# One transformer layer with a mixture of experts on one core: three float32r passes on split operands in place of two float32 passes in the shared gate and up products

## The reference

```python
x = _layernorm(x + attention(x))
normed = _layernorm(x, ln_w, ln_b); xf = normed.reshape(-1, 256)
logits = xf @ router_w
top_idx = argmax(logits); top_score = sigmoid(max(logits))
# routed: each token goes, scaled by top_score, through the expert top_idx
shared = silu(xf @ sh_gate) * (xf @ sh_up) @ sh_down     # 256 -> 512 -> 256
x = _layernorm(x + (x + routed + shared))
```

## Time and profile before

| | us |
|---|---|
| runs before (3): lowest, median, highest | 968.13, 968.39, 968.78 |
| span of the profiled execution, first to last instruction | 966.2 |
| median minus span | 2.2 |
| TensorE busy in the span | 942.9 (98%) |
| VectorE busy | 738.7 (76%) |
| ScalarE busy | 463.9 (48%) |
| GpSimd busy | 357.6 (37%) |
| blocks of the shared expert, first gate to first expert gate | 557.2 to 762.1 |

### The profile page before, as it was taken

The page is one execution under the profiler, slowest core; times in us unless marked ns, Lnnn a source line. Parts: engine busy times, 40 slices in busy tenths (PEclk is TensorE's granted clock), DMA queues, the critical chain, the costliest instruction groups (busy, mean ns, idle before and its releaser), DMA issues. The chain is left out here.

```text
span 966.2 us, 19079 instructions
## 1 busy us (share of the span) xinstructions
PE 942.9 (98%) x6068; PEld 526.2 (54%) x6068; DVE 738.7 (76%) x1835; ACT 463.9 (48%) x648; POOL 357.6 (37%) x475
## 2 busy tenths in 40 slices
PE   9999899999999999999999899999999999999996
PEld 5555433334344333433433256666665799947996
DVE  5889899999999899999996566666666467576564
ACT  2553466666766676677666722211212232364321
POOL 8995242222222222212222324333444233333334
PEclk9999999999999999999999999999999999999999
DMA  8797444446665464855621187333316232222321
GB/s 305 191 256 206 67 67 57 57 62 89 94 100 73 58 102 54 121 74 77 141 35 13 13 266 222 112 83 88 88 50 221 74 85 80 70 57 76 99 68 45
DMA packets 174815, 98.97 MB, mean 102 GB/s; under 512 B 132480, under 2 KB 161408, under 8 KB 171520
## 3 DMA queue, kind: packets, MB, share of 16 engines
q1 hardware_dynamic: 161344, 71.85, 39.0%
q10 hardware_dynamic: 8576, 12.58, 3.9%
q0 software_dynamic: 4800, 13.38, 3.7%
HBM read 65.05 MB, written 32.31 MB: 101 GB/s over the span
## 5 line engine op out<-in xcount | busy, mean ns | idle before, releaser
L1092 ACT ACTIVATE probs<-scores_ps 128x1024 f32<-128x1024 f32 (+3 forms) x384 | 289.7, 807 | 111.3 <-PE scores_ps L1033 108.5
L302 DVE TENSOR_REDUCE maxima<-max_ps 128x1 f32<-128x512 f32 (+2 forms) x352 | 227.1, 681 | 24.7 <-PE max_ps L260 18.6
L260 PE MATMUL max_ps<-k_stack,q_stack 96*128 96x512 bf16 (+3 forms) x768 | 221.7, 329 | 3.9 <-DVE maxima L297 1.1
L1171 POOL TENSOR_SCALAR_AFFINE_SELECT probs<-probs 128x512 f32<-128x512 f32 x128 | 81.3, 636 | 303.2 <-ACT probs L1092 302.4
L1033 PE MATMUL scores_ps<-q_stack,k_stack 99*128 99x512 bf16 (+3 forms) x768 | 182.6, 326 | 2.9 <-ACT probs L1092 1.3
L1053 PE MATMUL out_ps<-probs,v_ones 128*32 128x512 f32 (+3 forms) x1536 | 163.6, 498 | 3.5 <-POOL probs L1171 3.0
L260 PEld LDWEIGHTS max_ps<-k_stack,q_stack 96*128 96x128 bf16 x768 | 74.0, 96 | 156.7 <-DVE maxima L302 60.6
L297 DVE CUSTOM_DVE_ANT_0 masked_out<-max_ps,mask_wide 128x384 bf16<-128x384 f32 (+1 forms) x256 | 149.7, 620 | 11.6 <-PE max_ps L260 7.1
L1559 ACT ACTIVATE silu<-gate_ps 128x512 f32<-128x512 f32 x68 | 40.6, 597 | 211.8 <-PE gate_ps L1460 111.3
L1033 PEld LDWEIGHTS scores_ps<-q_stack,k_stack 99*128 99x128 bf16 x768 | 66.9, 98 | 65.2 <-ACT probs L1092 15.6
L1921 POOL DMA_INDIRECT out<-out_t,target_i x36 | 45.5, 1263 | 88.7 <-DVE out_t L1851 88.7
(11 more groups left out here) (210 smaller groups left out, 1244.0 us busy)
## 6 DMA issues: line engine op xcount, KB each, us to landing
k_stack<-k_parts SPq DMA_DIRECT2D x96, 128.0 KB, 4.3
q_stack<-q_parts SPq DMA_DIRECT2D x96, 128.0 KB, 7.2
q_parts<-parts SPq DMA_DIRECT2D x32, 192.0 KB, 3.2
k_parts<-parts SPq DMA_DIRECT2D x32, 192.0 KB, 3.2
sums_in<-expert_sums SPq DMA_DIRECT2D x31, 136.0 KB, 2.1
heads_rows<-heads_out SPq DMA_DIRECT2D x128, 32.0 KB, 1.9
res<-in_x SPq DMA_DIRECT2D x8, 512.0 KB, 4.6
heads_in<-heads_rows SPq DMA_DIRECT2D x64, 64.0 KB, 3.2
```

The source lines that it names most:

```text
L260: last = nc.tensor.matmul(part, self.q_stack[:ROWS, u.slot, h0 + k, t * P:(t + 1) * P], self.k_stack[:ROWS, u.slot, h0 + k, chunk * BLOCK: ...
L302: nc.vector.tensor_reduce(self.maxima[:, u.slot, chunk, h0:h0 + heads, t], self.bank("piece", u.i, n)[:, :heads * keys].rearrange("p (h k) ...
L1092: nc.scalar.activation(probs[:, s % RING, 2 * pair:2 * pair + 2, n0:], scores_ps[:, pair, :, n0:], ACT.Exp).then_inc(exp_done, 1)
L1171: nc.gpsimd.affine_select(out=tile, in_=tile, compare_op=ALU.is_ge, fill=0.0, base=0, pattern=[[0, GROUP], [1, P]], channel_multiplier=-1) ...
```

## The change

The shared weights are loaded into two spare tiles as before. GpSimd splits them during attention units 7 to 14, a quarter of one matrix per unit, at steps 10 and 11: a rounded copy (high) and the remainder (low), both as float32r. Each block's tokens are split too: `keep_xf` writes `xf_t` as before, then `take_xf_high` on ScalarE makes a rounded copy in `xf_split`, then `leave_xf_low` on GpSimd subtracts it from `xf_t`. For block 0 VectorE does all three in the last attention unit. Gate and up then run three matmuls per half of the channels: high x high, high x low and low x high (weight x token). Four tiles share memory in new ways (`xf_t` has one copy instead of two and serves as `rows_in` later, `hidden_t` and `sums_in` lie on the gate's and up's high parts, `row` moves into `feed`), and a `memset` of `row` goes.

```diff
+HIGH, LOW = 0, 1
+THREE = [(HIGH, HIGH), (HIGH, LOW), (LOW, HIGH)]
...
     def keep_xf(self, act, copy, i, batch, odd):
         act.wait_ge(self.xf_turned, i + 1)
-        wait(act, self.up_done, BT * (i - 1))
-        copy(self.xf_t[:, odd], self.front_ps[:]).then_inc(self.xf_t_kept, 1)
+        wait(act, self.routed, i)
+        copy(self.xf_t[:], self.front_ps[:]).then_inc(self.xf_t_kept, 1)
+
+    def take_xf_high(self, act, copy, i, batch, odd):
+        act.wait_ge(self.xf_t_kept, i + 1)
+        wait(act, self.up_done, BT * i)
+        copy(self.xf_split[:, HIGH].bitcast(F32R), self.xf_t[:]).then_inc(self.high_made, 1)
+
+    def leave_xf_low(self, eng, marker, subtract, i, batch, odd):
+        eng.wait_ge(self.high_made, i + 1)
+        wait(eng, self.up_done, BT * i)
+        stand(eng, marker)
+        subtract(self.xf_split[:, LOW].bitcast(F32R), self.xf_t[:], self.xf_split[:, HIGH],
+                 ALU.subtract).then_inc(self.low_made, 1)
...
-        nc.gpsimd.memset(self.row[:], 0.0).then_inc(self.const_step, 1)
...
+    def split_shared(self, pool, n, part):
...
+        if part == HIGH:
...
+            self.nc.gpsimd.tensor_copy(high.bitcast(F32R), loaded).then_inc(self.split_step, 1)
+        else:
...
+            self.nc.gpsimd.tensor_tensor(low.bitcast(F32R), loaded, high, ALU.subtract).then_inc(self.split_step, 1)
...
                     if (u.i, s) == OPEN["turn_xf"]:
                         f.keep_xf(dve, nc.vector.tensor_copy, 0, 0, 0)
+                        f.take_xf_high(dve, nc.vector.tensor_copy, 0, 0, 0)
+                        f.leave_xf_low(dve, f.dve_stood, nc.vector.tensor_tensor, 0, 0, 0)
...
+                    if s >= STEPS - 2 and 0 <= u.i - GROUPS - 3 < 2 * f.PIECES:
+                        f.split_shared(pool, u.i - GROUPS - 3, s - STEPS + 2)
...
+            def times_xf(to_ps, weights, n):
+                for c in range(DC):
+                    for weight, token in THREE:
+                        last = nc.tensor.matmul(to_ps, weights[weight][:, c, n * P:(n + 1) * P].bitcast(F32R),
+                                                f.xf_split[:, token, c].bitcast(F32R),
+                                                start=(c == 0 and (weight, token) == THREE[0]),
+                                                stop=(c == DC - 1 and (weight, token) == THREE[-1]))
+                return last
+
             def gate(i, n, odd):
-                pe.wait_ge(xf_t_kept, i + 1)
+                pe.wait_ge(f.high_made, i + 1)
+                pe.wait_ge(f.low_made, i + 1)
                 wait(pe, silu_made, IC * i + n - 1)
...
+                times_xf(gate_ps[:, n % 2], sh_gate, n).then_inc(gate_done, 1)
...
                 if nxt is not None:
                     f.keep_xf(act, nc.scalar.copy, i + 1, nxt, 1 - odd)
+                    f.take_xf_high(act, nc.scalar.copy, i + 1, nxt, 1 - odd)
...
                     scatter_sums(i - 1, 1 - odd, range(BT - 1))
+                f.leave_xf_low(pool, pool_stood, nc.gpsimd.tensor_tensor, i, None, odd)
                 scatter_rows(i, odd)
```

More of the change, by code:

```diff
@@ L22 @@
 F32 = mybir.dt.float32
+F32R = mybir.dt.float32r
 BF16 = mybir.dt.bfloat16
@@ L621 @@
     VEC_STEPS = 17
-    CONSTS = 15
+    CONSTS = 14
+    PIECES = 4
+    SUM_RING = 3
+    SPLITS_MADE = 2 * 2 * PIECES
     def __init__(self, nc, io, keep, scratch, b):
@@ L627, in __init__ @@
         self.n = 0
-        self.sh_gate = b.sb("sh_gate_sb", [P, DC, INNER])
-        self.sh_up = b.sb("sh_up_sb", [P, DC, INNER])
+        with ExitStack() as split_ctx:
+            split = Bufs(nc, split_ctx)
+            high = [split.sb(f"sh_{name}_high", [P, DC, INNER]) for name in ("gate", "up")]
+            low = [split.sb(f"sh_{name}_low", [P, DC, INNER]) for name in ("gate", "up")]
+        self.sh_gate, self.sh_up = zip(high, low)
+        self.hidden_t = b.sb("hidden_t", [P, 2, INNER])
+        self.sums = b.sb("sums_in", [P, self.SUM_RING, RECORD])
+        b.sb("up_high_end", [P, DC * INNER - self.SUM_RING * RECORD])
+        self.sh_loaded = [b.sb("sh_gate_sb", [P, DC, INNER]), b.sb("sh_up_sb", [P, DC, INNER])]
         self.router = b.sb("router_sb", [P, DC, self.QUAD])
+        self.split_step, self.high_made, self.low_made = b.sem("split_step"), b.sem("xf_high_made"), b.sem("xf_low_made")
         self.logits = b.sb("logits", [P, BT, self.QUAD])
@@ L645, in __init__ @@
         self.xf = b.sb("xf", [P, BT, D])
-        self.xf_t = b.sb("xf_t", [P, 2, DC, BLOCK])
-        self.row = b.sb("row", [P, 2, BT, D])
+        self.xf_t = b.sb("xf_t", [P, DC, BLOCK])
+        self.xf_split = b.sb("xf_split", [P, 2, DC, BLOCK])
         self.stats = b.sb("stats", [P, BT, 6])
@@ L762, in route @@
         for c in range(DC):
-            tokens = self.xf_t[:, odd, c].rearrange("p (t n) -> p t n", t=BT)
+            tokens = self.xf_t[:, c].rearrange("p (t n) -> p t n", t=BT)
             for q in range(0, P, self.QUAD):
@@ L938, in make_consts @@
         pool.wait_ge(self.const_step, self.CONSTS)
+    def split_shared(self, pool, n, part):
+        which, piece = divmod(n, self.PIECES)
+        width = DC * INNER // self.PIECES
+        high, low, loaded = [tile[:].rearrange("p c n -> p (c n)")[:, piece * width:(piece + 1) * width]
+                             for tile in (*(self.sh_gate, self.sh_up)[which], self.sh_loaded[which])]
+        if part == HIGH:
+            pool.wait_ge(self.ffn_in, 16 * 2)
+            stand(pool, self.pool_stood)
+            self.nc.gpsimd.tensor_copy(high.bitcast(F32R), loaded).then_inc(self.split_step, 1)
+        else:
+            pool.wait_ge(self.split_step, 2 * n + 1)
+            stand(pool, self.pool_stood)
+            self.nc.gpsimd.tensor_tensor(low.bitcast(F32R), loaded, high, ALU.subtract).then_inc(self.split_step, 1)
     def fill_tails(self, sp):
@@ L1007, in step @@
                 if u.i == GROUPS + 1:
-                    f.load_shared(sp, f.sh_gate, "sh_gate")
+                    f.load_shared(sp, f.sh_loaded[0], "sh_gate")
                 if u.i == GROUPS + 2:
-                    f.load_shared(sp, f.sh_up, "sh_up")
+                    f.load_shared(sp, f.sh_loaded[1], "sh_up")
                 if u.i in (GROUPS + 4, GROUPS + 6):
@@ L1208, in feed @@
     f = keep["front"]
-    ROW_RING, SUM_RING = 4, 3
+    ROW_RING, SUM_RING = 4, f.SUM_RING
     sh_gate, sh_up, x1, xf_t, place_i = f.sh_gate, f.sh_up, f.x1, f.xf_t, f.place_i
@@ L1217, in feed @@
     row_made, token_used = f.row_made, f.token_used
-    rows_scattered, sums_scattered, row = f.rows_scattered, f.sums_scattered, f.row
+    rows_scattered, sums_scattered = f.rows_scattered, f.sums_scattered
     with ExitStack() as ctx:
@@ L1223, in feed @@
         silu = b.sb("silu", [P, 2, INNER])
-        hidden_t = b.sb("hidden_t", [P, 2, INNER])
+        row = f.row = b.sb("row", [P, 2, BT, D])
+        hidden_t, sums = f.hidden_t, f.sums
         shared_t = b.sb("shared_t", [P, IC, BLOCK])
@@ L1248, in feed @@
         half_owner_i = b.sb("half_owner_i", [P, 2 * SPLITS], I32)
-        rows = b.sb("rows_in", [P, ROW_RING, D])
-        sums = b.sb("sums_in", [P, SUM_RING, RECORD])
+        rows = xf_t[:].rearrange("p c n -> p (c n)").rearrange("p (r d) -> p r d", r=ROW_RING)
         rows_t = f.out_sb[:].rearrange("p (o d) -> p o d", o=2)
@@ L1396, in _ @@
         def _(pe):
+            def times_xf(to_ps, weights, n):
[6 more added lines that the diff above has]
+                return last
             def gate(i, n, odd):
-                pe.wait_ge(xf_t_kept, i + 1)
+                pe.wait_ge(f.high_made, i + 1)
+                pe.wait_ge(f.low_made, i + 1)
                 wait(pe, silu_made, IC * i + n - 1)
[L1400 to L1403, removed]
+                times_xf(gate_ps[:, n % 2], sh_gate, n).then_inc(gate_done, 1)
             def up(i, n, odd):
                 wait(pe, hidden_made, IC * i + n - 1)
[L1407 to L1410, removed]
+                times_xf(up_ps[:, n % 2], sh_up, n).then_inc(up_done, 1)
             def down(i, t):
@@ L1544, in step @@
                 block_step(2 * batch + 1, 1, after, after)
-            pe.wait_ge(ffn_in, 32)
+            pe.wait_ge(f.split_step, f.SPLITS_MADE)
             by_batch(pe, step)
```

2 lines of the change are left out of this document (1 added, 1 removed).

## The result

| | before | after |
|---|---|---|
| median of 4 runs, us | 968.26 (967.28 to 968.78) | 972.42 (971.87 to 972.71) |
| span of the profiled execution, us | 966.2 | 970.8 |
| TensorE busy | 942.9 | 930.2 (96%) |
| VectorE busy | 738.7 | 753.0 (78%) |
| GpSimd busy | 357.6 | 381.3 (39%) |

The ratio is 1.0047, 95% interval 1.0036 to 1.0059: slower by about 4.5 us, half a per cent. The forecast was 965.2, faster, with a range up to 971.0. The time lies outside it, on the other side.

A forecast was written before the change was run, and what follows sets the result against it. The prediction took TensorE to bound the kernel, with VectorE's chain about a microsecond and a half behind. Its terms, 8.2 - 8.4 + 3.4 = 3.2 us faster, took 968.4 to 965.2 us, range 959 to 971.

The forecast's parts named there:

- TensorE's passes: Gate and up: 48 float32r passes of 0.216 us replace 32 of 0.429, 3.4 us less a block if nothing else bound.
- the second rival: Gate and up: float32r passes run two cycles a column, 0.429 us each, giving 1032 us; chance 0.10.
- What VectorE leaves of it: Second `down` behind VectorE's products: blocks 1 to 5 gain 7.4 us, with block 0's 0.84 together 8.2.
- The stand: `is_top` in `choose` stands until GpSimd's subtraction ends, making `count_ranks` 1.4 us later in six fronts: 8.4 us lost.
- The last two blocks: Blocks 6 and 7: gate of block 7 only about 0.4 us earlier, second `down` 2.8 to 4.4; gain taken as 3.4.
- The clock: TensorE in all blocks: full clock, 0.997 of 2.4 GHz, so a pass costs its columns; no loss priced.
- the splits of the weights: GpSimd in attention: 16 splits, at most 0.53 us each, at no cost; 8.5 us if the cover were gone.
- The rival with no stand: `choose` beside the subtraction: VectorE's small instructions slip in between, the 8.4 us stay, 956.8 us; chance 0.13.

The follow-up runs named there:

- e2: The changed kernel without the subtraction in blocks 1 to 7, block 0's low part of the tokens being used again; 956.21 us, ratio 0.9883.
- e3: As e2, but without the product with the tokens' low part, so two float32r passes per product instead of three; 958.32 us, ratio 0.9882.
- e8: The changed kernel with GpSimd's subtraction in blocks 1 to 7 replaced by a memset of the same tile to zero; 956.64 us, ratio 0.9883.
- e1: The changed kernel with one more wait: GpSimd's subtraction starts only when `choose` of the same front is through; 968.64 us, ratio 1.0008.
- e9: The changed kernel with three unread float32 matmuls ahead of each `count_ranks` of blocks 1 to 7; 969.20 us, ratio 1.0013.
- e4: The changed kernel with its copies and subtraction, but gate and up as one float32 matmul on the high parts; 988.15 us, ratio 1.0192.
- e6: The changed kernel with the subtraction on VectorE, behind `find_place` for blocks 1 to 6, behind `choose` for block 7; 957.70 us, ratio 0.9887.

## Why the prediction was wrong, point by point

**TensorE's passes.** Six took 1.39 us, 0.232 each, against 0.216 forecast and about 0.25 from which the second rival decides. About a column a cycle was right. By the Trainium skill's page "TensorE: Matmul & The Clock Gate", section "Weight-path perf modes", which the prediction cited, the array takes one element per cell per cycle whatever the element's width. The trace agrees within a tenth: 512 columns at 2.4 GHz would be 0.213 us, an estimate, and a pass took 0.232.

**What VectorE leaves of it.** Right in blocks 1 to 5: they are 1.74, 1.57, 1.17, 1.60 and 1.44 us shorter in e2 than before, 7.5 against the 7.4 forecast, and e3 shows that it is VectorE's chain that stops there. Only block 0 gained 0.2 in place of 0.84: its `times_wo` starts 0.63 us earlier, and 0.4 of that is lost behind it, where `up` waits 1.84 us for a product and then ran at half clock. In e3 the same block, at full clock, kept its earlier start whole (1.57 us earlier, 1.5 shorter), so the lower clock is the likely cause.

**The stand.** The mechanism was right, and shown by e2 and e8: `is_top` ends with the subtraction. By the Trainium skill's page "SBUF — State Buffer", section "Who interferes with whom", a GpSimd instruction that only writes does not hold a VectorE instruction with two inputs in SBUF, while copies and `tensor_scalar` can be held with one input too, in a two-port mode. e8's `is_top` (0.19 us beside the memset) agrees with the first; the 2.77 us of L906, and the 1.34 us of its like in e8 beside the memset, agree with the second, though no run shows in which mode they ran. The size was wrong. The forecast took 2.13 us for the subtraction, which is 2.34, and 1.4 for the stand; against e2 blocks 0 to 5 lose 1.54, 1.60, 1.81, 1.95, 1.81 and 1.78 (3.47 less the 1.69 of the slow `times_wo`), 10.5 us in place of 8.4. All lie within the bounds that were given, 0.9 to 2.0.

**The last two blocks.** This step failed with the largest difference. Its sentence "By then `choose` of block 7 is nearly over" was wrong: nearly over was not over, and a step on four columns stood for 2.77 us. The prediction looked at steps with two inputs in SBUF alone; the row at 742.09 above, of one with a single input, would have told it more. No wait for `choose` was priced there, and nothing covers one, since block 7 has no `times_wo` between `count_ranks` and the gate. But the wait by itself is dear only in part. The gate waits for the subtraction in any case, which ended at 746.84; in e1, where `choose` runs free, the gate follows on the subtraction within 0.11 us. So `choose` made the gate about 0.6 us later, an estimate from these rows. The larger part is what follows: passes at the lower clock. From block 6's first gate to the first expert gate it is 42.7 us, 0.9 more than before (41.8), where 3.4 less was forecast.

**The clock.** This is the term that turned the sign: the sum had it at nothing. "So a pass costs its columns" was read from the full clock of the kernel before and carried over, without a reason, to a kernel in which the prediction itself had TensorE wait ahead of every `count_ranks` and of block 7's gate. Before, TensorE waited at most 0.54 us at a time inside the blocks. 1.7 us of the loss are the `times_wo` from 719.02 (5.38 us in place of 3.70), and 2.8 are block 7's slow passes (19.20 us against 16.42 in e9): 4.5 together, more than the 3.2 that the forecast had to gain. Freeing `choose` would not have been enough: in e1 block 7's gate waited 2.32 us for the subtraction alone, and ran at half clock behind it.

The sum in the profiled executions: the forecast's span is 963.0, the one measured 970.8. Of the 7.8 us, about 4.3 are the last two blocks (2.8 of them the clock), 2.1 the stand, 1.7 the clock in `times_wo`, 0.5 the gain, less 0.7 for an attention that ended earlier: the splits of the weights cost nothing there, as forecast, though the subtraction of a quarter took 0.73 us, where at most 0.53 was said. By cause, the clock is the largest term with 4.5, and without it the kernel would have come out about where it was before; e9, at 1.0013, bears that out. The rival with no stand was right about what the kernel would be without it, 956.8 against 956.2. No rival had the waits and the lower clock together, which is what came.

What is not settled: which waits bring the lower clock. Waits of 1.64 to 2.05 us in blocks 0 to 4 did not bring it in the changed kernel, 1.85 in block 5 did; in e4 1.65 did, and 2.05 did not.

## What to carry to other kernels

When work moves to a free engine, ask whose instructions it holds up while it runs, and who waits for the smallest of those: here 2.3 us in each of seven blocks, on a GpSimd that is busy 39% of the time, cost 15.9 us in all, because a 0.19 us step of VectorE was what TensorE waited for next. The same subtraction on the busier VectorE, put into a wait that it already has and behind whatever feeds another queue, costs about 2 us at most (e6). And a wait priced at its length is priced too low where the waiting engine's clock can fall behind it.

## What the runs showed of the hardware that was not expected

- Which VectorE instructions stand beside a GpSimd subtraction that reads SBUF: two inputs in SBUF (`is_top` 1.78 us, `rank` times `chosen` 1.81), but also the `tensor_scalar` with one input of four columns (2.77). The reduction to `top` ran beside it in its usual time (0.19 us at 608.46, with the subtraction at work from 608.08), and so did the sums with one input in PSUM (e1: 0.18 and 0.16 us at 609.76 and 609.98, with the subtraction at work from 609.59).
- The `tensor_scalar` with one input stood beside GpSimd instructions that the steps with two inputs passed: 1.34 us beside a memset (e8), and 0.33 beside a scatter in every kernel whose GpSimd had no more to do there, the one before among them.
- A few matmuls without use in a wait kept the full clock and made the kernel faster (e9).
- In the profiled execution of e6 the half clock also came at the start of block 0, behind a wait of 1.16 us that the other profiles have too, at full clock.
